# A fused audio tower on one core: Newton halves in three places of each piece, other slots for the state-space steps and weight transpositions, and filler transpositions in the set-up

## What is computed

```python
fr = jnp.fft.rfft(x.reshape(B, C, 5, 200), axis=-1)
feats = jnp.concatenate([jnp.abs(fr), jnp.angle(fr)], axis=-1)      # 2 * 101
h = gelu(feats @ W1 + b1) @ W2 + b2                                 # 202 -> 808 -> 128, 320 rows per batch

inv_term = jnp.linalg.inv(I - 0.5 * dt * A)                         # 32 x 32
A_bar, B_bar = (I + 0.5 * dt * A) @ inv_term, dt * (inv_term @ B)
state = tanh(state @ A_bar.T + xn[t] @ B_bar.T)                     # 320 steps, xn = layernorm(h)
h = h + (states @ C.T + xn * D) @ W_out.T + b_out

z, r = sigmoid(...h2 @ Wwz.T), sigmoid(...h2 @ Wwr.T)               # GRU, width 256, 320 steps
c = tanh(xc[t] + (h2 * r) @ Ww.T); h2 = z * h2 + (1 - z) * c
h = h + sigmoid(h2 @ Wo.T + bo)
```

## Time and profile before

| | |
|---|---|
| median of 3 runs | 895.92 us (894.9 to 898.41) |
| profiled execution | 894.79 us, span 893.0 us |
| PE busy | 829.9 us (93%) |
| DVE busy | 578.6 us (65%) |
| ACT busy | 369.8 us (41%) |
| POOL busy | 89.7 us (10%) |
| mean granted clock of TensorE | 0.581 of full speed |

### The profile page before, as it was taken

One profiled execution on the slowest core, in us unless ns is written; L12 is line 12 of the kernel. 1 busy time (PEld: TensorE's weight loads), 2 busy tenths in 40 slices (PEclk: granted clock), 3 DMA queues, 4 the chain that ended last, 5 costly groups with the idle time before them and its releaser, 6 DMA issues.

```text
span 893.0 us, 40450 instructions
## 1 busy us (share of the span) xinstructions
PE 829.9 (93%) x17013; PEld 700.3 (78%) x17013; DVE 578.6 (65%) x3480; ACT 369.8 (41%) x2016; POOL 89.7 (10%) x205
## 2 busy tenths in 40 slices
PE   7889999989999999999999999999999998988875
PEld 5667666778888888888888888888888887877765
DVE  5243527376676776767767777677667777676654
ACT  5465766433343433433434334334333343343222
POOL 4212204110000000100000001000000000000000
PEclk6699999955555555555555555555555555555555
DMA  7100000000000000000000000000000000000000
GB/s 173 35 1 1 1 1 1 1 3 3 7 3 7 6 4 6 7 3 7 4 6 7 3 7 6 4 6 3 7 6 4 6 7 3 6 4 5 6 3 8
DMA packets 7452, 8.51 MB, mean 10 GB/s; under 512 B 1343, under 2 KB 6557, under 8 KB 7271
## 3 DMA queue, kind: packets, MB, share of 16 engines
q1 hardware_dynamic: 6965, 5.92, 2.8%
q0 software_dynamic: 256, 0.01, 0.0%
q10 hardware_dynamic: 50, 0.00, 0.0%
HBM read 4.62 MB, written 1.31 MB: 7 GB/s over the span
## 4 chain that ended last, share of the span: by engine, by line
PE 85%; ACT 6%; DVE 4%; issue 3%; DMA 1%; POOL 0%; POOLq 0%
PE ps L1511 42%; PE ps L1517 11%; PE ps L1313 8%; PE ps L1372 5%; PE ps L1423 3%; PE ps L1387 3%; PE ps L1525 3%; DVE h_hi L478 2%; PE ps L1431 2%; ACT addend L866 2%; PE ps L1295 1%; PE ps L1302 1%; PE ps L1283 1%; PE ps L1231 1%; PE ps L1247 1%
## 5 line engine op out<-in xcount | busy, mean ns | idle before, releaser
L1511 PE MATMUL ps<-h_hi,w_first 128*128 128x8 f16 x2552 | 267.3, 170 | 28.4 <-DVE h_hi L478 28.0
L1511 PEld LDWEIGHTS ps<-h_hi,w_first 128*128 128x128 f16 x2552 | 219.9, 104 | 90.9 <-DVE h_hi L478 90.9
L1511 PE MATMUL ps<-h_hi,w_rest 128*128 128x8 f16 x5104 | 276.3, 168 | 0.0
L1511 PEld LDWEIGHTS ps<-h_hi,w_rest 128*128 128x128 bf16 x5104 | 240.6, 105 | 0.1
L856 ACT ACTIVATE tanh_r<-ps 128x16 f32<-128x16 f32 x320 | 58.6, 183 | 252.3 <-PE ps L1517 251.7
L1517 PE MATMUL ps<-h_lo,w_first 128*128 128x8 f16 x2560 | 160.0, 168 | 0.1
L1511 PE MATMUL ps<-rh_hi,w_first 128*128 128x8 f16 x1276 | 136.6, 173 | 12.1 <-DVE rh_hi L1133 1.0
L1511 PEld LDWEIGHTS ps<-rh_hi,w_first 128*128 128x128 f16 x1276 | 109.6, 104 | 39.0 <-DVE rh_hi L1133 1.3
L1511 PE MATMUL ps<-rh_hi,w_rest 128*128 128x8 f16 x2552 | 138.6, 168 | 0.0
L478 DVE TENSOR_TENSOR_SCAN h_hi<-coef,addend 128x32 f16<-128x32 f32 x320 | 73.1, 228 | 85.7 <-ACT addend L866 85.7
L1511 PEld LDWEIGHTS ps<-rh_hi,w_rest 128*128 128x128 bf16 x2552 | 121.8, 105 | 0.0
(11 more groups left out here) (211 smaller groups left out, 1421.6 us busy)
## 6 DMA issues: line engine op xcount, KB each, us to landing
x_sb<-in_x SPq DMA_DIRECT2D x4, 500.0 KB
out<-res SPq DMA_DIRECT2D x20, 64.0 KB, 2.0
W_sb<-in_L_tok_W SPq DMA_DIRECT2D x1, 606.0 KB
W_sb<-in_L_tok_W SPq DMA_DIRECT2D x1, 384.0 KB
wnat<-in_L_ffn_Wwr SPq DMA_DIRECT2D x1, 256.0 KB, 5.4
wnat<-in_L_ffn_Wwz SPq DMA_DIRECT2D x1, 256.0 KB, 11.2
wnat<-in_L_ffn_Ww SPq DMA_DIRECT2D x1, 256.0 KB, 10.5
wunat<-in_L_ffn_Wur SPq DMA_DIRECT2D x1, 128.0 KB, 6.9
```

Source lines behind the costliest of these rows:

```text
L1511: mm(gate(c, j, g, m), w[:, m * 128:(m + 1) * 128], state[:, k * NB:(k + 1) * NB], start=False, stop=False, skip_group_check=True)
```

## The change

Of the Newton halves and steps, only the slots are changed, not their number. With the change, n = 0 holds 20 halves (8 to 27), n = 1 nineteen (28 to 46), n = 2 fifteen (47 to 61), n = 3 eighteen (62 to 79), and n = 4 none. In the odd half groups slot 1 is now in use. The state-space steps begin in piece 6 of n = 4 (three), go on in n = 5 (nineteen, all three slots) and end in n = 6 with slots 0 and 2 of pieces 0 to 4 (ten). The products of `BAR_AT` stand in piece 4 of n = 4 instead of 5. The weights' blocks go to pieces 5 and 6 of n = 4 and pieces 0, 1 and 4 of n = 5. (PE transposes a block in the piece before the one listed.) The second quarter's spectrum stands one piece earlier in n = 0. In the set-up PE makes 26 more of the transpositions at the start and 78 more between the products there (`busy`), whose results nobody reads. One wait on `im_read` is added in the set-up; the two calls of `wait_newton` name the same kind of half as before.

```diff
 NEWTON = 40
-WARM = 26
+WARM = 52
+BUSY = 6
 EARLY = 8
...
-SCAN_FROM = 5, 0
-BAR_AT = 4, 5
-
-WEIGHTS_AT = {(5, 1): 0, (5, 2): 1, (5, 3): 2, (5, 4): 3, (5, 5): 4}
+SCAN_FROM = 4, 6
+BAR_AT = 4, 4
+
+WEIGHTS_AT = {(4, 5): 0, (4, 6): 1, (5, 0): 2, (5, 1): 3, (5, 4): 4}
...
-SPECTRA_LATE = 2
+SPECTRA_LATE = 1
...
         def blocked(n, m, slot):
-            if slot == 1 and n % 2:
+            if slot == 1 and n == NG - 1:
                 return True
             if n in (2, 4) and slot and m in (XT_PIECE, SKIP_PIECE):
                 return True
             if n in (2, 4) and (m, slot) == (SQRT_PIECE + 2, 0):
                 return True
-            if (n, m, slot) in ((1, 0, 0), (1, 1, 0)):
+            if (n, m, slot) in ((0, SQRT_PIECE + 2, 1), (2, SQRT_PIECE + 1, 1), (4, SQRT_PIECE + 1, 1)):
                 return True
             return n in (1, 3, 5) and (m, slot) in ((ATAN_PIECE + 1, 2), (ATAN_PIECE + 2, 0))
...
-                    if blocked(n, m, slot):
-                        continue
-                    if taken < HALVES:
+                    if taken < HALVES and not blocked(n, m, slot):
                         SLOTS[n, m, slot] = taken
                         taken += 1
-                    if (n, m) >= SCAN_FROM and scanned < 2 * CH:
+                    if (n, m) >= SCAN_FROM and (n < SCAN_FROM[0] + 1 or not blocked(n, m, slot)) and scanned < 2 * CH:
                         SCANS[n, m, slot] = scanned
                         scanned += 1
...
+            def busy(count, b):
+                for _ in range(count):
+                    tr(bank(b)[:, 0:128], ident[:], ident[:])
+
             pe.wait_ge(consts, 1)
-            for _ in range(WARM):
-                tr(bank(6)[:, 0:128], ident[:], ident[:])
+            busy(WARM, 6)
             transposes(0, 0)
             transposes(0, 1)
+            busy(BUSY, 6)
             pe.wait_ge(su_dve, 2)
...
             spectra(0, 1)
+            busy(2 * BUSY, 0)
             pe.wait_ge(su_dve, 11)
...
             mm(bank(2)[:, 0:3 * DM], ones_row[:], vec_rows[:].rearrange("p a d -> p (a d)"),
                start=True, stop=True).then_inc(su_pe, 1)
+            busy(BUSY, 0)
             newton(1)
             tr(bank(5)[:, 0:128], Wout_sb[:], ident[:]).then_inc(su_pe, 1)
+            busy(BUSY, 0)
             newton(2)
             transposes(1, 0)
             for i in range(3, 6):
+                busy(BUSY, 4)
                 newton(i)
             pe.wait_ge(rows_in, 16 * 8)
             tr(bank(4)[:, 0:32], bias_rows[:], ident[0:32, 0:32]).then_inc(bias_psum, 1)
             for i in range(6, EARLY):
+                if i == 6:
+                    pe.wait_ge(im_read, 2)
+                busy(2 * BUSY, 7)
                 newton(i)
+            busy(BUSY, 7)
             pe.wait_ge(su_act, 6)
...
                         if m == 0:
-                            wait_newton(SLOTS[n, 0, 0] - 1)
+                            wait_newton(max(i for key, i in SLOTS.items() if key < (n, 0, 0)))
                         spectra(g, m // 2)
                     if n and m == XT_PIECE:
                         if shared:
-                            wait_newton(SLOTS[n, m, 0])
+                            wait_newton(max(i for key, i in SLOTS.items() if key < (n, m, 1)))
                         transpose_x(n - 1)
```

## The result

The changed kernel takes 898.58 us (median of 20 executions, 896.44 to 908.12) where the kernel before takes 895.96 (20 executions on the same chip). The ratio is 1.0062, 95% interval 1.0043 to 1.0082: it is slower, by 0.6%. Six of the 20 executions lie in a group of their own at 906 to 908 us, and the ratio counts them; the mean of the other 14 is 1.003 of the mean before. One of the experiments shows what happens in such an execution.

A forecast was written before the change was run, and what follows sets the result against it. GRU loop (715.34 of 893.0 us, half clock) carried over; only the PE-busy front of 177.66 us moves. Set-up and n = 0 to 6: -0.3 - 4.6 - 1.0 - 0.5 + 1.7 + 1.8 - 0.4 - 3.7 = -7.0, giving 888.9 us, range 883.5 to 896.5.

The forecast's parts named there:

- the part on n = 1: Half group n = 1: wait and slow clock gone, Newton chain longer; sum -1.0 us, bounds -4 and +1.5.
- the new wait at (1,0): Start of n = 1: half 28 waits 1.65 us behind ACT's gelu table load, gelu and copy of half 27.
- after 1.13 and 1.70 us it stayed at 1.00: PE waits in n = 3 and n = 5 before the change, cited against the clock falling again within the set-up.
- The prediction's own sign of being wrong: Wrong if the clock record shows 0.50 after 9 us, the loop changes, or three-place half groups do not lengthen.
- B_bar's wait: First state-space step at (4,6,0): PE waits some 2.2 us for DVE's B_bar; n = 4 in all +1.8 us.
- The first: Rival: clock falls again within the set-up, about 3 us of the gain go, 892 us; chance 0.20.
- The third: Rival: waits at (0,6) to (1,0), in n = 3 and at (4,6,0) reach upper bounds; 894 us; chance 0.10.
- The second rival: Set-up fillers run at the half clock throughout, n = 0 gains nothing: +2.4 us, 898.3 us; chance 0.08.
- The set-up's sum: Set-up: DVE's chain -1.05 us against uncovered fillers and delayed first transpositions; sum -0.3, bounds -1.5 and +1.
- -5.9 for wait and clock: n = 1: the 2.49 us wait for add_rows goes, and 3.4 us come back from the slow clock.
- +4.9 for the Newton chain: n = 1: three halves in a row +1.1 us, piece 3 +0.5, pieces 5 and 6 +0.4, square root's stalls +2.9.
- the two new waits: n = 5: 0.95 us for the last block's copy at the sixteenth step, 0.75 behind the arctangent at (5,3,1).

The follow-up runs named there:

- a_fill1: Changed kernel plus 12 filler transpositions ahead of the first Newton half of n = 1, at (1,0): 891.6 us, 0.9998 of before.
- a_fill14: Changed kernel plus 12 fillers at (1,0) and 16 ahead of the first state-space step in (4,6): 889.83 us, 0.9966 of before.
- b_fill1: Kernel before plus the set-up's fillers and 20 more in n = 1 ahead of the down product that waits for add_rows: 891.47 us, 0.9922 of before.
- b_warm26: b_fill1w with 26 instead of 52 transpositions at the start, those between the products kept: 886.91 us, 0.9921 of before.
- b_fill1w: b_fill1 with the weights' blocks moved to the changed kernel's places: 888.92 us, 0.9897 of before.
- a_again: The changed kernel run once more, nothing altered: 899.6 us, 1.0034 of before; its profiled execution took 906.15 us.
- a_fill145: a_fill14 plus 8 fillers at (5,3) and 6 ahead of step 16 at (5,5): 890.46 us, 0.9961 of before.
- experiment 12: b_fill1w with the second quarter's spectrum one piece earlier in n = 0, Newton slots giving way to the root: 887.33 us, 0.9909 of before.

## Why the prediction was wrong

The forecast was 888.9 us, with a range from 883.5 to 896.5; 898.58 lies above it. The two traces and the runs settle the 10.3 us between the GRU's forecast shift (-7.0) and the measured one (+3.28):

| step | us | shown by |
|---|---|---|
| clock falls behind the wait at (1,0) | +4.4 | n = 1: 26.01 after, 21.60 in a_fill1 |
| clock falls behind the wait at (4,6) | +1.6 | n = 4: 24.91 after, 23.32 in a_fill14 |
| set-up | +1.6 | 52 transpositions in 8.83 us |
| n = 1 at the full clock | +1.35 | 21.60 against 20.25 |
| n = 3 | +0.8 | 19.46 against 18.7 |
| n = 5 | +0.6 | 19.33 against 18.73 |
| n = 0, 2, 4 (full clock), 6 | 0.0 | -4.5, -0.56, +1.75, -3.69 |

**The step that failed** is in the part on n = 1. It gives the slow 3.4 us of before back because add_rows no longer waits, and charges the new wait at (1,0) only with its own length. The mechanism of that wait was right (ACT's gelu load ahead of the copies of half 27), and so was its size, 1.48 us against 1.65. Its consequence was missing: the clock. The text had the rule at hand, "after 1.13 and 1.70 us it stayed at 1.00", and took it for a threshold. The length of a wait does not decide: the clock fell after 1.48 us at 54.43 and after 1.07 us in b_fill1, and stayed after 1.65 us in b_warm26 and 1.07 us in b_fill1w. Two waits that did no harm were no evidence that a third would do none. The prediction's own sign of being wrong, 0.50 after 9 us, came in n = 1 and n = 4.

The same holds at (4,6): B_bar's wait is 1.99 us where 2.2 was forecast, and n = 4 at the full clock is +1.75 where +1.8 was. Only the clock behind it was not in the sum, though 2.2 us is longer than the 1.70 which the text had seen do no harm.

**The rivals** had both halves of the cause, apart. The first let the clock fall, but only in the set-up, where it was dismissed by the same threshold (in the profiled execution the clock held there; in a_again, the same kernel, it fell for 3.4 us). The third let the new waits come to their upper bounds, but priced them without the clock. What came is their combination: the waits at their forecast size, and the clock as their price. The second rival gave 898.3, a figure close to the measured one, for a mechanism that the clock of 1.00 in the set-up and n = 0 rules out.

**Sizes.** The set-up's sum took the pace of the first transpositions from one execution; where it doubles differs from execution to execution. The 52 took 8.83 us here and 7.20 in a_fill145, and the set-up 29.77 and 28.16, near the forecast 28.2; the other runs with 52 lie between. Most of the +1.6 is therefore not the change's. In n = 1 the forecast's two terms were both too large: -5.9 for wait and clock (measured -1.9 for the clock by 19.37 against 21.25, and -1.1 for the spectrum by experiment 12), and +4.9 for the Newton chain (measured +3.3). In n = 3 the pieces 0 to 2 cost 1.4 where 1.3 was forecast, the pair at the arctangent 0.7 instead of 0.5; pieces 5 and 6, 0.2 longer each than laid out, are the rest. In n = 5 the two new waits are near the forecast (0.84 and 0.67 us against 0.75 and 0.95), but what leaves it gave less: in b_fill1w a wait of 0.99 us for a gelu stands where the 1.70 us for the copy were. The rest of n = 5 is open. n = 6 came out right by two misses that cancel: up to the first up of piece 5 it gave 1.69 us where 1.35 was forecast, from there to the bank set 2.00 where 2.35 was.

**Right** were n = 0 and with it the fillers' effect, n = 2, n = 4 without the clock, the sum of n = 6, and the direction of n = 3. The GRU loop was carried over unchanged; it was 1.1 us longer in this execution, and between 714.0 and 717.3 us in all profiled ones, so a single execution's total has some 3 us of play from the loop alone.

## What to carry to other kernels

When a change moves a wait, price the clock behind the wait as well as the wait: here 1.5 us of idle cost another 4.4, and a handful of dead transpositions in the same gap took that away. Here a chain of small dependent products, whose copies share ACT's queue with gelus and table loads, gained nothing from a third place in a piece. Separate the parts of such a change: its fillers and its moved weights gained by themselves, and the moved slots, with the earlier spectrum, gave that back even at the full clock.

## What the runs showed of the hardware

The time at the lower clock level after a fall varied much more than the wait before it, with PE busy throughout: 3.4 us (140.8 to 144.2) and 24 us (138.2 to 162.1) after the same wait of 1.99 us in two executions of one kernel, 13.6 and 10.2 us after the same wait of 1.48 us (the changed kernel's execution above and a_again's), 34 us after two waits of under 1 us, 3.4 us again after one of 0.47 us. That parts the one profiled execution of the upper group from the one of the lower: a_again's profiled span is 6.9 us longer than the changed kernel's above (904.3 against 897.4), and its n = 5 alone is 7.65 us longer (26.98 against 19.33). The others of the upper group were not profiled; their mean clock (0.584 or 0.585, where all others have 0.590 to 0.594) agrees. What sets the time at the lower level stays open.

The GRU loop, the same instructions at 0.50 throughout, took 714.20, 715.34, 716.46 and 717.26 us in four profiled executions (a_fill14, before, after, b_fill1w); eight of the fourteen lie between 714.0 and 714.2, three near 717.2. The fronts do not explain it: b_fill1 and b_fill1w, with the same code in the loop and on one chip, have 714.13 and 717.26. Two kernels whose fronts differ by less than 3 us can't be ordered by one execution's total. The stages at the full clock repeat to 0.1 us (all but the set-up), and so the stage view orders them.
